# A two-layer graph transformer on one core: first stage reordered, its row stores carried into the linear attention, 16 edge columns counted in the attention's prologue

## What is computed

```python
def _layernorm(x, axis=-1, eps=1e-05):
    m = jnp.mean(x, axis=axis, keepdims=True)
    v = jnp.var(x, axis=axis, keepdims=True)
    return (x - m) / jnp.sqrt(v + eps)
...
    edge_index = jnp.stack([src, dst])
    xn = _layernorm(x, axis=-1)
    x = x + _L0_gnn_ref(xn, edge_index, ...) + _L0_mix_ref(xn[None], ...)[0]
...
# in _L0_mix_ref: h = x + _performer_attn(_layernorm(x, ln1_g, ln1_b), qkv_w, ...)
        q = _feature_map(qkv[0], w_orf)      # exp(x w - |x|^2 / 2) / sqrt(M), M = 384
        k = _feature_map(qkv[1], w_orf)
        k_sum = jnp.sum(k, axis=2)
        D = jnp.einsum('bhnm,bhm->bhn', q, k_sum)[..., None] + EPSILON
        ktv = jnp.einsum('bhnm,bhnc->bhmc', k, v)
        out = jnp.einsum('bhnm,bhmc->bhnc', q, ktv) / D
```

## Time and profile before

| What | us |
|---|---|
| median of 3 runs | 3432.07 (3430.57 to 3433.05) |
| profiled execution, its own time | 3428.94 |
| its span | 3427.2 |
| DVE starts the second stage | 85.27 |
| the barrier at the second stage's end opens, SP starts the third stage's loads | 561.1, 561.82 |
| first and last scatter-add on POOL start | 140.90 and 556.26 |

### The profile page before, as it was taken

The page is one execution under the profiler, slowest core; times in us unless marked ns, Lnnn a source line. Parts: engine busy times, 40 slices in busy tenths (PEclk is TensorE's granted clock), DMA queues, the critical chain, the costliest instruction groups (busy, mean ns, idle before and its releaser), DMA issues. The chain is left out here.

```text
span 3427.2 us, 50208 instructions
## 1 busy us (share of the span) xinstructions
PE 2888.5 (84%) x17656; PEld 2481.1 (72%) x17656; DVE 2312.9 (67%) x4167; ACT 1449.7 (42%) x2424; POOL 462.6 (13%) x327
## 2 busy tenths in 40 slices
PE   1999996967999998887988599868999977887794
PEld 1999995745788998777986233248999955777794
DVE  4665652735851553998664888657788858998775
ACT  3464552213112332555243577521546512554345
POOL 2287885200000000000002310000000000000000
PEclk9999998988999999999999699979999988999997
DMA  8333325694211653623131311253311077212301
GB/s 249 85 49 57 47 33 134 213 220 98 77 44 56 184 174 98 170 66 80 35 75 29 98 40 45 55 167 120 72 46 45 23 178 212 76 50 78 84 21 47
DMA packets 255535, 319.45 MB, mean 93 GB/s; under 512 B 97933, under 2 KB 179342, under 8 KB 255208
## 3 DMA queue, kind: packets, MB, share of 16 engines
q1 hardware_dynamic: 177576, 272.11, 29.4%
q0 software_dynamic: 77760, 44.83, 6.6%
HBM read 236.35 MB, written 79.53 MB: 92 GB/s over the span
## 5 line engine op out<-in xcount | busy, mean ns | idle before, releaser
L195 POOL DMA_INDIRECT adj_d<-edge_val,edge_off x160 | 332.5, 2078 | 184.6 <-DVE edge_off L183 100.0
L3191 DVE TENSOR_TENSOR expert_wgel<-expert_gel,expert_wps 128x417 f32<-128x417 f32 (+1 forms) x384 | 203.0, 584 | 57.0 <-PE expert_wps L3116 46.6
L2102 PE MATMUL gat00att_ops<-gat00att_h,gat00att_p 125*125 x1600 | 198.2, 280 | 48.4 <-DVE gat00att_p L2076 48.4
L2102 PE MATMUL gat10att_ops<-gat10att_h,gat10att_p 125*125 x1600 | 195.9, 279 | 48.4 <-DVE gat10att_p L2076 48.4
L2102 PEld LDWEIGHTS gat00att_ops<-gat00att_h,gat00att_p 125*125 125x125 f32 x1600 | 183.8, 189 | 63.0 <-issue 63.0
L2102 PEld LDWEIGHTS gat10att_ops<-gat10att_h,gat10att_p 125*125 125x125 f32 x1600 | 184.1, 192 | 60.8 <-issue 60.8
L3163 ACT ACTIVATE expert_gel<-expert_hps 128x417 f32<-128x417 f32 (+1 forms) x384 | 193.5, 519 | 64.2 <-DVE expert_wgel L3191 52.5
L577 PE MATMUL perf_wide<-y_lo,perf_qk_hi 128*128 128x416 f32 (+1 forms) x432 | 154.9, 359 | 24.7 <-DVE perf_qk_lo L759 24.4
L1275 PE MATMUL fc_ps<-y_lo,fc_w_hi 128*128 128x512 f32 (+1 forms) x432 | 154.6, 358 | 22.3 <-DVE fc_w_lo L1317 22.3
L1428 PE MATMUL fc_ops<-fc_w_hi,fc_x_lo 128*125 128x384 f32 x480 | 163.7, 341 | 7.1 <-DVE fc_w_lo L1480 7.1
L715 ACT ACTIVATE perf_kphi<-perf_wide,perf_lnm 125x384 f32<-125x384 f32 (+1 forms) x180 | 95.7, 630 | 172.5 <-PE perf_wide L601 171.6
(11 more groups left out here) (491 smaller groups left out, 7932.0 us busy)
## 6 DMA issues: line engine op xcount, KB each, us to landing
fc_w<-in_L_mix_fc_w SPq DMA_DIRECT2D x96, 384.0 KB
adj_d<-edge_zero POOLq DMA_DIRECT2D x22, 546.9 KB
gat00proj_adj<-adj_d POOLq DMA_DIRECT2D x20, 546.9 KB, 7.0
perf_keys<-keys_d SPq DMA_DIRECT2D x20, 437.5 KB
gat00att_sh<-shift_d SPq DMA_DIRECT2D x16, 546.9 KB
sh<-shift_d SPq DMA_DIRECT2D x16, 546.9 KB
perf_w<-in_L_mix_qkv_w SPq DMA_DIRECT2D x18, 384.0 KB
perf_w<-in_L_mix_W_qkv SPq DMA_DIRECT2D x18, 384.0 KB
```

The costliest lines, as they stand in the source:

```text
L195: edges.nc.gpsimd.indirect_dma_start(out=edges.adj_flat[u].rearrange("(n a) -> n a", a=1), out_offset=bass.IndirectOffsetOnAxis(ap=edges.o ...
L2102: ins = pe.matmul(ops[0:TP, u, b, t * w:(t + 1) * w], p[:, s, (t0 + t) * TP:(t0 + t + 1) * TP], h[:, s, bass.ds(hd, 1), :], start=(s == 0 ...
L3191: dve.tensor_tensor(wgel[:, q % W, 0:cn], gel[:, q % 3, 0:cn], wps[:, q % 3, 0:cn], ALU.mult).then_inc(wgel_done, 1)
```

## The change

In the first stage DVE takes the statistics of two pairs before it normalises the first, and from then on stays two pairs ahead; the small edge weights are computed early, and the low parts of a pair follow one pair later. ACT's order follows. The tile x moves into a buffer that lives on into the second stage (`LateRows`), where `kphi` and `qphi` are laid over it; the stage no longer waits for the row stores. ACT waits for them in the second stage, before its pair loop. After the second pair's store SP waits for the stored keys and loads chunks 0 and 1, into buffers that also live on. In the second stage DVE counts these two chunks (16 columns) in the prologue, behind the first bias copy; SP loads chunks 2 and 3 at the prologue's end; each count in the pair loop is of the chunk two higher, and the last head pair that counts (i = 2, u = 0) counts two chunks instead of four.

```diff
@@ -124,10 +124,12 @@
         self.key = sb("edge_key", [TP, EC])
+        self.keys = sb("edge_keys", [TP, self.SLOTS, self.COLS * TP])
...
         self.cleared = nc.alloc_semaphore("edge_cleared")
+        self.keys_ld = [nc.alloc_semaphore(f"edge_keys_ld{u}") for u in range(self.SLOTS)]
@@ -142,6 +144,21 @@
+    def load_keys(self, sp, k, u):
+        n = self.COLS * TP
+        move_rows(sp, self.keys[:, u, :], row_bcast(self.keys_d[bass.ds(k * n, n)], TP), self.keys_ld[u])
+class LateRows:
+    def __init__(self, nc, name, sb):
+        self.room = sb(f"{name}_room", [128, NT * D])
+        self.x = self.room[0:TP, :].rearrange("p (t d) -> p t d", t=NT)
+        self.stored, self.stored_n = nc.alloc_semaphore(f"{name}_stored"), 32 * (NT // 2)
@@ -149,20 +166,18 @@
         self.edges, cols = edges, edges.COLS
-        self.keys = S.sb("keys", [TP, edges.SLOTS, cols * TP])
+        self.keys, self.keys_ld = edges.keys, edges.keys_ld
...
         self.offset = S.sb("offset", [TP, 2, cols])
-        self.keys_ld = [S.sem(f"keys_ld{u}") for u in range(edges.SLOTS)]
...
         S.sems.append(edges.cleared)
+        S.sems.extend(edges.keys_ld)
...
-        n = self.edges.COLS * TP
-        if not (isinstance(k, int) and k < self.edges.SLOTS):
-            sp.wait_ge(self.summed, (k - self.edges.SLOTS + 1) * self.edges.COLS)
-        move_rows(sp, self.keys[:, u, :], row_bcast(self.edges.keys_d[bass.ds(k * n, n)], TP), self.keys_ld[u])
+        sp.wait_ge(self.summed, (k - self.edges.SLOTS + 1) * self.edges.COLS)
+        self.edges.load_keys(sp, k, u)
@@ -212,7 +227,7 @@
         key_rows = S.sb("key_rows", [128, 2, TP])
-        x = S.sb("x", [TP, NT, D])
+        x, stored = late.x, late.stored
@@ -249,8 +264,10 @@
                     move_rows(sp, tokens(normed_d)[:, tiles, :], x[:, tiles, :], stored)
-                sp.wait_ge(key_st, 32)
-                sp.wait_ge(stored, 32 * pairs)
+                    if g == 1:
+                        sp.wait_ge(key_st, 32)
+                        for u in range(edges.SLOTS):
+                            edges.load_keys(sp, u, u)
@@ -299,18 +316,19 @@
                 root(0)
-                act.wait_ge(gains_ld, 32)
-                root2(0)
...
                 act.copy(key_rows[0:rest, 1, :], kps[0:rest, 1, 0:TP]).then_inc(key_kept, 1)
+                act.wait_ge(gains_ld, 32)
+                root(1)
                 for g in range(pairs):
-                    if g + 1 < pairs:
-                        root(g + 1)
+                    root2(g)
+                    if g > 0:
+                        keep(2 * g - 1)
+                    if g + 2 < pairs:
+                        root(g + 2)
                     keep(2 * g)
-                    if g + 1 < pairs:
-                        root2(g + 1)
-                    keep(2 * g + 1)
+                keep(NT - 1)
@@ -371,19 +389,18 @@
                 take_stats(0)
-                take_root(0)
-                second_norm(0)
+                take_stats(1)
+                edge_weights()
                 for g in range(pairs):
-                    if g + 1 < pairs:
-                        take_stats(g + 1)
-                        low_part(2 * g)
-                        take_root(g + 1)
-                        low_part(2 * g + 1)
-                        second_norm(g + 1)
-                    else:
-                        low_part(2 * g)
-                        edge_weights()
-                        low_part(2 * g + 1)
+                    take_root(g)
+                    if g + 2 < pairs:
+                        take_stats(g + 2)
+                    second_norm(g)
+                    if g > 0:
+                        low_part(2 * g - 2)
+                        low_part(2 * g - 1)
+                low_part(NT - 2)
+                low_part(NT - 1)
@@ -428,8 +445,13 @@
         v = S.sb("v", [TP, NT, 4, vw])
-        kphi = S.sb("kphi", [TP, NT, m])
-        qphi = S.sb("qphi", [128, mb_n, N])
+        if late is not None:
+            kphi = late.room[0:TP, 0:NT * m].rearrange("p (t m) -> p t m", t=NT)
+            qphi = late.room[:, NT * m:NT * m + mb_n * N].rearrange("p (b n) -> p b n", b=mb_n)
+            S.sems.append(late.stored)
+        else:
+            kphi = S.sb("kphi", [TP, NT, m])
+            qphi = S.sb("qphi", [128, mb_n, N])
@@ -496,11 +518,8 @@
                     if counted is not None:
-                        counted.load(sp, i * 8 + 4 * u + n, n % 2)
-                if counted is not None:
-                    counted.load(sp, 0, 0)
-                    counted.load(sp, 1, 1)
+                        counted.load(sp, i * 8 + 4 * u + n + 4, n % 2)
@@ -509,6 +528,9 @@
                 load_qk(1)
+                if counted is not None:
+                    counted.load(sp, 2, 0)
+                    counted.load(sp, 3, 1)
@@ -517,7 +539,7 @@
                     load_qk(i * 2 + 2)
-                    for n in range(2, 6):
+                    for n in range(4):
@@ -525,15 +547,12 @@
                         load_features(i * 2 + 2)
-                    for n in range(2, 6):
+                    for n in range(4):
...
                     load_features(HP - 1)
-                if counted is not None:
-                    for n in (2, 3):
-                        load_keys(HP // 2 - 1, 0, n)
@@ -738,6 +757,8 @@
                 rounded(0)
+                if late is not None:
+                    act.wait_ge(late.stored, late.stored_n)
@@ -848,9 +869,11 @@
                     def count(n):
-                        if counted is not None and not (isinstance(i, int) and u == 1):
-                            counted.count(dve, i * 8 + 4 * u + n, n % 2, (i * 8 + 4 * u + n - n % 2) // 2 if isinstance(i, int)
-                                          else i * 4 + 2 * u + n // 2)
+                        last_chunk = isinstance(i, int) and (u == 1 or n >= 2)
+                        if counted is not None and not last_chunk:
+                            chunk = i * 8 + 4 * u + n + 2
+                            nth = i * 4 + 2 * u + n // 2 + 1
+                            counted.count(dve, chunk, n % 2, nth)
@@ -901,6 +924,9 @@
                     set_bias(0)
+                if counted is not None:
+                    counted.count(dve, 0, 0, 0)
+                    counted.count(dve, 1, 1, 0)
@@ -3664,13 +3690,14 @@
             edges = Edges(nc, lambda s, shape, dt=F32: sb(ctx, s, shape, dt), keys_d, adj_flat)
+            late = LateRows(nc, "xn", lambda s, shape: sb(ctx, s, shape))
...
             norm_stage(nc, ident, inp["src"], inp["dst"], inp["lower"], edges, 1e-5,
-                       inp["x"], xn_d, inp["L0_mix_ln1_g"], inp["L0_mix_ln1_b"], parts, first)
+                       inp["x"], xn_d, inp["L0_mix_ln1_g"], inp["L0_mix_ln1_b"], parts, first, late)
...
                             inp["L0_mix_w_orf"], True, 384, HD ** -0.25, 1e-8, attn_d,
-                            edges=edges)
+                            edges=edges, late=late)
```

More of the change, by code:

```diff
@@ L200, in add, with norm_stage @@
             pool.wait_ge(added[u], EC // sets * 16)
-def norm_stage(nc, ident, src, dst, lower, edges, eps, x_d, normed_d, gain_cols, shift_cols, yT, first):
+def norm_stage(nc, ident, src, dst, lower, edges, eps, x_d, normed_d, gain_cols, shift_cols, yT, first, late):
     pairs = NT // 2
@@ L228, in norm_stage @@
         var_ready, std_ready, var2_ready, std2_ready = (S.sem(s) for s in ("var_ready", "std_ready", "var2_ready", "std2_ready"))
-        normed, y_ready, turned, full_ready, high_done, low_done, stored = (S.sem(s) for s in (
-            "normed", "y_ready", "turned", "full_ready", "high_done", "low_done", "stored"))
+        normed, y_ready, turned, full_ready, high_done, low_done = (S.sem(s) for s in (
+            "normed", "y_ready", "turned", "full_ready", "high_done", "low_done"))
         with nc.Block() as block:
@@ L398, in load, with performer_stage @@
             sp.dma_start(self.w[:, k], kblocks(self.w_d)[:, :, c:c + 128]).then_inc(self.loaded, 16)
-def performer_stage(nc, name, y_parts, first, w_d, bias_cols, vbias_d, feat_d, per_head, m, scale, eps, out_d, edges=None, scan=None):
+def performer_stage(nc, name, y_parts, first, w_d, bias_cols, vbias_d, feat_d, per_head, m, scale, eps, out_d, edges=None, late=None, scan=None):
     mb_n = m // 128
```

## The result

The changed kernel takes 3417.0 us (median of 5, 3415.47 to 3423.51) beside 3432.89 for the kernel before (median of 5, 3430.57 to 3436.07): ratio 0.9958, with a 95% interval from 0.9946 to 0.997, which is 14.4 us less (10.3 to 18.5; the two medians by themselves differ by 15.9). The profiled span is 3413.7 us beside 3427.2. Forecast were 3422.5 us, a saving of 9.6, with a range from 3415 to 3431.

What follows compares the result with a forecast made beforehand. POOL's clearing traffic was taken to bound the first stage, POOL's late scatter-adds to end the second. +3.8 + 0.7 - 14.1 = -9.6 us against the median 3432.07 gave 3422.5 us, range 3415 to 3431.

Steps and rivals of the forecast that it cites:

- Rival B: First stage: POOL's DRAIN does not hold it, so it closes near 58 us; total 3392 us, chance 0.05.
- Part 1: First stage, new order on DVE and ACT: DVE ends near 58 instead of 75.2, hidden by the clearing; 0 us.
- Part 2: First stage's end: row stores no longer waited for by SP, the wait moving to ACT in the next stage; 0 us.
- Part 3: First stage: loading two key chunks puts 1.0 MB more before the clearing's end; +3.8 us, bounds -1 to 11.9.
- Part 4: Second stage's prologue: DVE counts 16 columns in idle room of 5.6 us for 5.46; 0 us, at most 1.2.
- Rival D's mild form: Key loads cost 8 us and prologue casts the full 1.4; -4.7 us, total 3427.4; chance two thirds of 0.12.
- Part 5: Second stage: POOL's scatter-adds start at 98.1 instead of 140.90, so SP's wait at the end barrier goes; -14.1 us.
- rival C: Second stage: adds slow down beside loads, above 2.83 us each, so POOL stays last; 3460 to 3540 us, chance 0.05.
- Part 6: Second stage's prologue: DVE's casts slow while POOL generates descriptors beside them; +0.7 us, bounds 0 to 1.4.
- Rival D's hard lock: Prologue: 7 exposed casts each stand behind a 2.0 us add, 14 us; total 3435.8; chance one third of 0.12.

Runs made afterwards that it cites:

- g1: Changed kernel, but POOL clears only the first matrix copy in the first stage and SP the second in the next stage's prologue: 3395.8 us, 0.9887.
- e1: Kernel before with only DVE's and ACT's new order in the first stage; stores still waited for, keys loaded and counted as before: 3430.3 us, 0.9994.
- e4: Changed kernel with the last three row stores held back until DVE is through, after 55 us: 3420.2 us, 0.9956.
- e3: Changed kernel with the old order of DVE and ACT in the first stage, stores and key loads as changed: 3421.2 us, 0.9961; repeat 3412.5 us.
- e6: Changed kernel, but POOL waits for three counted chunks instead of one before its first add: 3434.6 us, 0.9999.
- r_after: The changed kernel run once more, nothing altered: 3420.6 us.

## Why the prediction was right, and where it was not

**What bounds the first stage: right.** POOL's DRAIN ends it in every kernel, with DVE idle for 26 us, and g1 moves it with the bytes. Rival B, by which the stage would have closed near 58, is refuted. The Trainium skill ("Perfetto Trace Analysis", section on the DMA instruction, SWDGE) is right in what it says: the last clearing transfer's row ends at 42.0 us, and the data moves for another 37. But the engine that issued it does not leave the stage until they have landed.

**Part 1, the order is worth 0: the cover held, a side effect was missed.** DVE ends at 55.1 (58 forecast: the 4 us that the first y was to lose were not lost) and e1 shows no gain. With the key loads beside it, though, the new order shortens the clearing by about 4 us (83.2 beside 87.3). I had treated the DMA rate as given by the bytes alone. With the new order it is higher at nearly the same busy share, 338 to 347 GB/s in 20 to 48 us instead of 316 and 303. Why is open: e4 excludes the time of the last three stores as the cause, and idle engines are excluded by the stretch in which the gain falls. That the transfers in it are a better mix, by the first two stores for one, was not tested.

**Part 2, the stores at 0: right.** ACT's wait for them in the second stage never shows, not even with the stores issued after 55 us.

**Part 3, the key loads: this is the term that failed in the sum.** With the order left alone it is +2.6 us (e3 and its repeat), where I had put +3.8: right in sign, somewhat large. I had priced them at the rate of loads that run alone (263 GB/s); they ran beside the clearing, in stretches that moved up to 405. Rival D's mild form had put 8 us on them. But the forecast added it to a first stage of 84.4 and expected the DRAIN's end between 86 and 90; it came at 80.6, 84.3 and 83.3, 82.7 in the mean, 2.0 below the kernel before. The two together, loads and order, are -2.0 instead of +3.8. In the profiled pair it is -3.8, of which nearly 2 are that execution's luck. With executions from three chips and no common chip for all, even the -2.0 is not firm.

**Part 4, 16 columns at 0.** The two chunks took 5.1 us instead of 5.46 (86.73 to 91.85), and the square came after them with no idle time left. The room was used up. The cost is about 1 us by e6, less than the 2 us by which single executions differ.

**Part 5, POOL starts earlier: right, -14.1 forecast.** The barrier wait went from 14.3 to 0.2. The steps came out so: first add 8.9 us behind DVE's start of the stage (98.1 - 89.1 = 9.0 forecast), chunk 2 waited for 1.09 us (4.5 forecast), last add over at 518.18 (520 forecast), SP 26 us later. The adds were 2.67 us each, and 2.72 in r_after (435.5 / 160), beneath the 2.83 from which POOL would be last again: rival C is refuted.

**Part 6, +0.7: not refuted.** The casts grew from 0.77 to 1.11 and 1.04 us a pair, and to 1.22 in r_after, just above the 1.14 of the earlier trace rows that the upper bound was made of. SP's path through the stage grew by about 0.4 us, which is within the scatter. Rival D's hard lock, by which a cast stands behind an add's 2.0 us, is refuted: no cast took that long. The exclusive lock that the Trainium skill states ("SBUF — State Buffer", section "Who interferes with whom") shows here as +0.27 to +0.45 us on a pair of casts and no more.

**The sum.** Means over the executions at hand give the first stage -2.0 and the second -11.7 (463.9 beside 475.6), -13.7 together, inside the -10.3 to -18.5 that the timed runs give. Forecast were -9.6. The first stage came out 5.8 us below its forecast (+3.8) and the second 1.7 above (-13.4), so two misses partly cancel. The range held, but the measured median of 3417.0 lies only 2 us above its lower end, and it was Part 3's upper side that the range had been made wide for.

## What to carry to other kernels

Ask for every stage which engine's DRAIN ends it, not which engine is busy. Where it is the one that issued bulk transfers, reordering the busy engines buys only idle time, and moving bytes that nobody needs yet behind the barrier buys time (20 us here, until the busy engines were nearly the next limit). A chain that is last at a later barrier by 14 us is best shortened at its start: the work ahead of its first link was there early enough. And profile both kernels more than once, and on the same chip, before a difference of 4 us in one stage gets a cause.

## What the runs showed of the hardware

- POOL's DRAIN at a stage's end lasts until its own transfers have landed: 44.0 to 50.9 us for 12.5 MB of clearing, 30.1 and 32.9 us for half of it. It ends 1.1 to 2.0 us behind the last packet of POOL's queue; POOL generates only in its first 3 to 6 us. SP's DRAIN in the same place took 0.2 us (at 47.3 in the changed kernel) although SP's queue had packets until 58.3, so it did not wait for its queue.
- Nearly the same share of busy DMA engines can mean 291 GB/s (0.97, 60 to 72 us before) or 398 (1.02, 36 to 42 us after). Share 1.0 says that they have work, not how fast it goes.
- SP can be held by issuing: 12 transfers that clear 6.25 MB took it 18.55 us of issue time. Here this was harmless: SP's next transfer went out at 87.70, and the stage kept its length.
- The changed kernel ended its clearing at 80.6, 84.3 and 83.3 us in three executions; at least two chips are among them, so chance and chip are not told apart.
